# A cross-attention lookup and a two-pass soft mixture of experts on one Trainium2 core: clamped indices, a three-bank routing loop and a bias carried by a weight row

## What is computed

```python
x = x + jnp.tanh(g_xattn[0]) * _L0_xattn_ref(_layernorm(x), itok_S_0_31, ctx_1024)
x = x + jnp.tanh(g_ffn[0]) * _L0_ffn_ref(_layernorm(x), phi_w, phi_b, expert_w, expert_b)

def _L0_xattn_ref(x, layer_idx, weight):
    w = weight[layer_idx]                       # one 128x128 matrix per position
    return jnp.einsum('bsd,sod->bso', x, w)

def _L0_ffn_ref(x, phi_w, phi_b, expert_w, expert_b):
    logits = (jnp.einsum('tzd,ed->tze', x, phi_w) + phi_b).reshape(t, z, n, p)  # n=64, p=32
    D = jax.nn.softmax(logits, axis=3)
    C = jax.nn.softmax(logits, axis=2)
    X_tilde = jnp.einsum('tznp,tzd->npd', D, x)
    X_tilde = jnp.tanh(normalised(jnp.clip(X_tilde, -33000.0, 65000.0)))
    Y_tilde = jnp.einsum('npd,ndH->npH', X_tilde, expert_w) + expert_b[:, None, :]
    return jnp.einsum('tznp,npH->tzH', C, Y_tilde)
```

## Time and profile before

| | |
|---|---|
| median of three runs | 2147.64 us |
| the three runs | 2143.88, 2147.64, 2164.28 us |
| the profiled execution, its own time | 2142.48 us |
| its span in the trace | 2140.7 us |
| mean granted TensorE clock | 0.894 |
| busy: PE / DVE / ACT / POOL | 1713.7 / 1334.7 / 1188.4 / 683.0 us |
| stages A, B1, M, B2 (about) | 0 to 128, 129 to 384, 384 to 425, 425 to 745 us |

### The profile page before, as it was taken

The page is one execution under the profiler, slowest core; times in us unless marked ns, Lnnn a source line. Parts: engine busy times, 40 slices in busy tenths (PEclk is TensorE's granted clock), DMA queues, the critical chain, the costliest instruction groups (busy, mean ns, idle before and its releaser), DMA issues. The chain is left out here.

```text
span 2140.7 us, 40008 instructions
## 1 busy us (share of the span) xinstructions
PE 1713.7 (80%) x12924; PEld 1252.7 (59%) x12924; DVE 1334.7 (62%) x3429; ACT 1188.4 (56%) x4072; POOL 683.0 (32%) x636
## 2 busy tenths in 40 slices
PE   3549999699999839999688865799649998649994
PEld 2425555377877616666487754545526676528883
DVE  4189999377777646667567757312446676674444
ACT  2149999178888618778544432334238888423333
POOL 3035555134444431212034421001300110156774
PEclk9879999599999969999899977799769999659997
DMA  3320000010000024333000022000033432301113
GB/s 109 71 99 1 1 0 1 17 35 1 1 0 1 17 63 109 77 90 100 25 1 0 0 79 83 3 0 0 6 93 95 99 88 68 125 12 46 50 52 138
DMA packets 49332, 99.25 MB, mean 46 GB/s; under 512 B 8842, under 2 KB 16332, under 8 KB 47556
## 3 DMA queue, kind: packets, MB, share of 16 engines
q1 hardware_dynamic: 44548, 87.68, 14.7%
q0 software_dynamic: 4608, 9.32, 1.4%
HBM read 68.14 MB, written 28.77 MB: 45 GB/s over the span
## 5 line engine op out<-in xcount | busy, mean ns | idle before, releaser
L585 ACT ACTIVATE B_E<-B_logits,B_m 128x32 f32<-128x32 f32 (+1 forms) x1792 | 360.2, 362 | 24.1 <-DVE B_m L554 22.6
L592 POOL TENSOR_TENSOR B_E<-B_E,B_r 128x512 f32<-128x512 f32 x256 | 267.7, 1046 | 316.8 <-DVE B_r L573 316.8
L1235 ACT ACTIVATE L_E<-L_sc,L_negm 128x128 f32<-128x128 f32 x1024 | 299.7, 405 | 122.2 <-DVE L_negm L1150 121.7
L1150 DVE TENSOR_REDUCE L_negm<-L_sc 128x4 f32<-128x512 f32 x256 | 174.2, 683 | 127.9 <-PE L_sc L1303 120.2
L554 DVE TENSOR_REDUCE B_m<-B_logits 128x16 f32<-128x512 f32 (+1 forms) x256 | 171.2, 669 | 56.5 <-PE B_logits L548 53.8
L1301 PE MATMUL L_sc<-KS,L_QS 128*128 128x512 f32 x256 | 142.0, 555 | 65.6 <-DMA L_QS<-L_qsplit 53.9
L568 DVE TENSOR_REDUCE B_r<-B_E 128x16 f32<-128x512 f32 (+1 forms) x256 | 172.8, 675 | 11.9 <-ACT B_E L585 10.1
L545 PE MATMUL B_logits<-B_phihi,B_xhi 128*128 128x512 f32 x256 | 156.2, 610 | 22.5 <-ACT B_E L585 10.6
L1243 ACT ACTIVATE L_PT<-L_pt 128x512 f32<-128x512 f32 x256 | 166.9, 654 | 0.6 <-PE L_pt L1311 0.6
L1311 PE MATMUL L_pt<-ident,L_E 128*128 128x128 f32 x1024 | 157.1, 276 | 1.6 <-ACT L_PT L1243 1.6
L1311 PEld LDWEIGHTS L_pt<-ident,L_E 128*128 128x128 f32 x1024 | 123.4, 142 | 24.1 <-ACT L_E L1235 2.0
(11 more groups left out here) (344 smaller groups left out, 3819.3 us busy)
## 6 DMA issues: line engine op xcount, KB each, us to landing
KS<-L_ksplit SPq DMA_DIRECT2D x192, 64.0 KB
L_QS<-L_qsplit SPq DMA_DIRECT2D x48, 256.0 KB, 3.9
F_w<-in_F_w SPq DMA_DIRECT2D x4, 2048.0 KB, 8.5
ew<-in_expert_w SPq DMA_DIRECT2D x1, 4096.0 KB, 14.6
L_cT<-in_ctxT SPq DMA_DIRECT2D x16, 256.0 KB, 4.7
L_ksplit<-L_khi SPq DMA_DIRECT2D x16, 256.0 KB, 2.0
L_ksplit<-L_klo SPq DMA_DIRECT2D x16, 256.0 KB, 2.4
L_qsplit<-L_qhi SPq DMA_DIRECT2D x16, 256.0 KB, 2.7
```

The lines of the kernel that those rows point to most:

```text
L585: ins = nc.scalar.activation(e[:, cols], self.bank(w)[:, cols], ACT.Exp, bias=self.m[:, w % 4, g:g + 1])
L592: self.st.nc.gpsimd.tensor_tensor(e, e, self.r[:, w % 2, :].unsqueeze(2) .to_broadcast([128, self.ng, self.size]), ALU.mult).then_inc(self ...
L1150: nc.vector.tensor_reduce(negm[:, k % 4, :], sc[k % 2][:].rearrange("p (h k) -> p h k", h=NHG), AX.X, ALU.max, negate=True).then_inc(s["ma ...
L1235: ins = nc.scalar.activation(e[:, h * 128:(h + 1) * 128], sc[k % 2][:, h * 128:(h + 1) * 128], ACT.Exp, bias=negm[:, k % 4, h:h + 1])
```

## The change

- Stage A: DVE clamps the indices to 0..31 and multiplies them by 128 once (`itoc`). PE loads 16 values at a time, with no check and no multiplication.
- Both routing passes: units carry one number k = 0..127, everything is written out with no hardware loop, and three logits banks are used as k modulo 3. DVE normalises the next group one sequence per unit (after units 5 to 8 in B1, 3 to 6 in B2). PE transposes after unit 11, ACT splits after unit 12, DVE makes the low half after unit 14.
- B2 gets a ring of eight, `delay` 2 and `LAG` 4, and DVE's finish is spread over units 8 to 11.
- B2's bias matmul is gone. A normalised row sums to zero, so feature 0 may be replaced by 1 when its weight row is subtracted from all rows and the bias put in its place. SP loads the weight row broadcast (`bc`) and the bias at the start of stage M; POOL clears one row of `bc` and subtracts it in four pieces, ahead of the power. The bias parts for B2 in stage A are gone.

```diff
--- before.py
+++ after.py
...
+            v.wait_ge(s["tok_in"], 16)
+            steps.link(nc.vector.tensor_scalar(itoc[:], itok[:], 0, B - 1, ALU.max, ALU.min))
+            nc.vector.tensor_scalar(itoc[:], itoc[:], D, None, ALU.mult).then_inc(s["tok_ready"], 1)
...
-            for h in range(S // 8):
-                _, toks = nc.values_load_multi_w_load_instructions(itok[0:1, 8 * h:8 * h + 8], engines=[mybir.EngineType.PE],
-                                                                   min_val=0, max_val=B - 1)
+            for h in range(S // 16):
+                _, rows = nc.values_load_multi_w_load_instructions(
+                    itoc[0:1, 16 * h:16 * h + 16], engines=[mybir.EngineType.PE], min_val=0, max_val=(B - 1) * D,
+                    skip_runtime_bounds_check_because="VectorE has clamped them")
...
-                                               ctxT[:, bass.ds(toks[4 * (k % 2) + i], 1), :].rearrange("p a o -> p (a o)"),
+                                               table[:, bass.ds(rows[4 * (k % 4) + i], D)],
...
+    def vector_ones(self):
+        for x in self.xn:
+            self.st.nc.vector.memset(x[:, :, 0:1], 1.0)
...
+        q, bank, last = k % NQ, self.bank(k)[:], k - len(self.banks)
+        nc, cols = self.st.nc, slice(q * 512, (q + 1) * 512)
+        if last >= 0 and self.shifted(last):
+            eng.wait_ge(self.diff_done, self.shifts(last))
+        elif last >= 0:
+            eng.wait_ge(self.exp_done, last + 1)
...
-        nc.tensor.matmul(bank, xhi, self.lo[:, cols], start=False, stop=False)
-        nc.tensor.matmul(bank, p.ones16[:], self.bias3[:, cols], start=False, stop=True).then_inc(self.logits_ready, 1)
+        ins = nc.tensor.matmul(bank, xhi, self.lo[:, cols], start=False, stop=self.bias3 is None)
+        if self.bias3 is not None:
+            ins = nc.tensor.matmul(bank, p.ones16[:], self.bias3[:, cols], start=False, stop=True)
+        ins.then_inc(self.logits_ready, 1)
...
-                    if w == LAG and more:
+                if n + 1 < NG:
+                    if w == LAG:
                         v.wait_ge(probs_used, n * UG + soft.RING)
-                        front.vector(v, n + 1, 1 - u)
-                    if w == UG - 4 and more:
-                        front.vector_low(v, n + 1, 1 - u)
+                    if LAG <= w < LAG + GB:
+                        front.vector(v, n + 1, (n + 1) % 2, [w - LAG])
+                    if w == UG - 2:
+                        front.vector_low(v, n + 1, (n + 1) % 2)
...
+            sp.dma_start(bc[:], d["phiT_slots"][0:1, :].to_broadcast([128, NE_L0])).then_inc(bc_in, 16)
+            sp.dma_start(p.phiT[1][0:1, :], d["phi_b_slots"]).then_inc(bias_row_in, 16)
...
+            g.wait_ge(bc_in, 16)
+            nc.gpsimd.memset(bc[0:1, :], 0.0).then_inc(row_set, 1)
+            g.wait_ge(row_set, 1)
+            g.wait_ge(bias_row_in, 16)
+            for q in range(4):
+                cols = slice(q * 512, (q + 1) * 512)
+                nc.gpsimd.tensor_tensor(p.phiT[1][:, cols], p.phiT[1][:, cols], bc[:, cols], ALU.subtract)
             g.wait_ge(var_ready, 1)
...
-    LAG = 3
+    LAG, DELAY = 4, 2
...
-        soft = SoftUnit(st, NL, ct_ready, p.phiT[1], p.bias3[1], 4)
+        soft = SoftUnit(st, NL, ct_ready, p.phiT[1], None, 4, 8, DELAY, 3)
...
+                    if 3 <= w < 3 + GB:
+                        front.vector(v, n + 1, (n + 1) % 2, [w - 3])
+                    if w == UG - 2:
+                        front.vector_low(v, n + 1, (n + 1) % 2)
+                if n:
+                    if w == 8:
+                        mark = add(n - 1)
+                    if w == 9:
+                        steps.need(mark)
+                        mark = tail.row_stats(v, n - 1, (n - 1) % 2, steps)
...
```

More of the change, by code:

```diff
@@ L602, in stage_b1 @@
     LAG, DELAY = 5, 2
+    NU = NG * UG
     with Stage(nc, "B1") as st:
@@ L622, in _ @@
             credit(g, (soft.probs_ready, 2))
-            over_groups_skewed(g, lambda n, u, first, more: [soft.gpsimd(g, n * UG + w, w) for w in range(UG)])
+            for k in range(NU):
+                soft.gpsimd(g, k)
         @block.vector
@@ L654, in _ @@
                     front.scalar(a, 0, 0)
-            def group(n, u, first, more):
-                for w in range(UG):
-                    soft.scalar_exp(a, n, w)
-                    if w == UG - 6 and more:
-                        if not first:
-                            a.wait_ge(soft.logits_ready, n * UG)
-                        front.scalar(a, n + 1, 1 - u)
-            over_groups_skewed(a, group)
+            for k in range(NU):
+                n, w = k // UG, k % UG
+                soft.scalar_exp(a, k)
+                if w == UG - 4 and n + 1 < NG:
+                    if n:
+                        a.wait_ge(soft.logits_ready, n * UG)
+                    front.scalar(a, n + 1, (n + 1) % 2)
         @block.tensor
@@ L814, in _ @@
             credit(g, (soft.probs_ready, 2))
-            def group(n, u, first, more):
-                for w in range(UG):
-                    soft.gpsimd(g, n * UG + w, w)
-                    if w == 10 and not first:
-                        tail.gpsimd(g, n - 1, 1 - u)
-            over_groups_skewed(g, group)
+            for k in range(NU):
+                soft.gpsimd(g, k)
+                if k % UG == 13 and k > UG:
+                    tail.gpsimd(g, k // UG - 1, (k // UG - 1) % 2)
             tail.gpsimd(g, NG - 1, 1)
@@ L839, in finish @@
                     ALU.mult, ALU.add))
-            def group(n, u, first, more):
-                for w in range(UG):
-                    soft.vector(v, n, w, not (first and w == 0))
-                    if w == 4 and more:
-                        v.wait_ge(ct_ready, n * UG + soft.RING)
-                        front.vector(v, n + 1, 1 - u)
-                    if w == UG - 4 and more:
-                        front.vector_low(v, n + 1, 1 - u)
-                    if w == 8 and not first:
-                        finish(n - 1, 1 - u)
@@ L857, in _ @@
+            for k in range(NU - DELAY, NU):
+                soft.vector_sum(v, k)
+                soft.vector_inverse(v, k)
+            steps.need(add(NG - 1))
+            tail.vector(v, NG - 1, 1, steps, None)
         @block.scalar
@@ L924, in _ @@
-            over_groups_skewed(t, group)
-            for w in range(UG, UG + LAG + 1):
-                if w < UG + LAG:
-                    turn((NG - 1) * UG + w - LAG, w - LAG)
-                combine((NG - 1) * UG + w - LAG - 1, w - LAG - 1, 1)
+            for k in range(NU):
+                n, w = k // UG, k % UG
+                if w == 0:
+                    t.wait_ge(front.halves, n + 1)
+                cols = slice(w // NQ * 128, (w // NQ + 1) * 128)
+                soft.tensor_logits(t, k, (front.hi[n % 2][:, cols], front.lo[n % 2][:, cols]), p)
+                if k >= LAG:
+                    turn(k - LAG)
+                if k == LAG + 1:
+                    t.wait_ge(Yt_in, 16)
+                if k > LAG:
+                    combine(k - LAG - 1)
+                if w == UG - 5 and n + 1 < NG:
+                    front.tensor(t, n + 1, (n + 1) % 2, False)
@@ L932 @@
+            for k in range(NU, NU + LAG + 1):
+                if k < NU + LAG:
+                    turn(k - LAG)
+                combine(k - LAG - 1)
 NHG = 4
```

261 lines of the change are left out of this document (122 added, 139 removed).

## The result

The changed kernel took 2069.99 us, the median of four runs (2057.71 to 2083.59), beside 2150.22 us for the kernel before (four runs, 2143.88 to 2164.28). The ratio is 0.9609, with a 95% interval of 0.9567 to 0.9652: faster by 80.2 us. The profiled execution took 2057.71 us, its span is 2055.6 us and the mean granted clock 0.895.

What follows compares the result with a forecast made beforehand. PE was taken to bound A (its sequencer), B1 narrowly and B2, with M waiting for POOL's power. -34.8 - 8.0 + 4.9 - 40.6 + 0.2 = -78.3 us gave 2064.2, raised to 2066; range 2054 to 2088.

Steps and rivals of the forecast that it cites:

- Stage A, -34.8: Stage A's lookup, without checks and multiplications on PE's sequencer, has ACT's last emptying near 66 us, 34.8 us earlier.
- 12 slow positions: Stage A's slow beginning: 12 positions at 0.43 us each, 5.2 us, before the steady 0.22 us a position.
- The seven further loads I cost at nothing: Stage A: PE's loads after the first hide because the sequencer runs ahead; otherwise 8 us come back.
- The lock in each unit: Rival, chance 0.10: in B1 POOL's product holds up each normalisation, making B1 16 us slower and the total 2090 us.
- Stage B1, -8.0: Single normalisations slip in ahead of POOL and PE's 1.10 us hole goes in seven groups: B1 8 us shorter.
- the banks go round by three: B1's logits banks used in turns of three, stated with the spread normalisations and given no time of its own.
- ACT with its 218.6 us holds the banks: The low end for B1: ACT's work, or a late low half, leaves a gain of nothing.
- Stage M, +4.9: POOL's new work ahead of the power makes it start at 398.2 instead of 393.35, 4.9 us more.
- I take 392: Stage M: the time the broadcast lands, chosen between 390.1 at the earliest and 394.5.
- Four subtractions go by POOL's product, 1.05 us each: Stage M: POOL's four subtractions of 512 ahead of the power take 4.2 us.
- Stage B2, -40.4 with the +0.2: B2 without the bias matmul loses 29.2 us, and 11.4 us of waits go; memsets and drain add 0.2.
- The rival that ACT sets the unit: Rival, chance 0.18: in B2 ACT's 2.10 us exceeds PE's 2.04 in unshifted units, making the total 2076 us.

Runs made afterwards that it cites:

- b1_one_piece: The changed kernel with B1's four normalisations of the next group again in one piece after unit 5; stage B1 took 257.70 us against 249.34.
- after_again: The changed kernel measured once more, nothing edited: 2089.2 us, ratio 0.9671 to the kernel before; stage M took 47.49 us.
- m_power_first: The changed kernel with POOL taking stage M's power first, clearing and subtracting after it; stage M took 36.68 us against 39.33.
- b1_old_banks: The changed kernel with B1's low half two units earlier and its banks in the old order 0, 1, 0, 2; stage B1 took 247.06 us.

## Why the prediction was right, and where it wasn't

The forecast of 2066 us lies 4.0 under the median of 2070; the range held it; no rival came true. What it named as the cause was borne out in each stage, but it put no price on the new order of the banks and didn't see the clock in M. How near the total came is partly luck, since the stages behind B2 alone took between 1387 and 1439 us in the profiles. Step by step:

- **Stage A, -34.8: right, -34.5.** PE's first matmul was put at 35.0 and came at 34.96, ACT's last emptying at 65.7 and came at 66.07. Two terms of it missed in opposite ways: 12 slow positions were to cost 2.5 us over the steady pace, and the first 32 took 1.3 us over it; a position takes 0.233 us and not 0.22, 1.6 us over all 128. "The seven further loads I cost at nothing" held nearly: a load of 16 values is 1.7 us long, more than twice that of eight, but 16 positions of PE's work are 3.7. The halved loads, which stand there beside the checks, were no help: with eight values a load stage A is 1.2 to 3.0 us shorter.
- **The lock in each unit: did not happen.** All 28 normalisations took 0.25 us. The row of group 6 with DVE 0.16 us ahead of POOL told this rightly (the kernel after has 169.71 against 169.87 us at such a place), and b1_one_piece shows the price where they aren't spread, 8.4 us. The rival's price was too high all the same: it gave a held normalisation 0.26 + 1.05 = 1.31 us, and the longest took 1.12 to 1.14, so "one product longer" is not what the earlier trace rows say.
- **Stage B1, -8.0: right mechanism, too large; -5.8.** The hole of 1.10 us went. The step that failed is "the banks go round by three", which I had put beside the pieces without a price. It stood among the ends only ("ACT with its 218.6 us holds the banks"). It costs 2.3 us against the old order with the low half early. With both of these B1 is 247.06 us, 8.0 less than before, which is the forecast; so the miss of 2.2 us lies in this step.
- **Stage M, +4.9: mis-sized, +6.5 at the same level over the expert matmuls.** "I take 392" for the broadcast was too early: POOL's clearing starts 8.2 us after the issue, and I had given it 6.6 (other profiles: 7.3 to 7.9). "Four subtractions go by POOL's product, 1.05 us each" was too cheap: they start 1.22 us apart, 0.7 us in all. The stage's own ends, 2.9 and 7.4, held it. The levels are not wholly equal, though: in before PE's first transposes of the stage ran at the lower one too, 3.64 us against 1.94 in after_again. m_power_first, where they took 1.94 us too, has its power 0.9 us sooner after the stage's start than before; with that the cost is nearer 7.4.
- **What stage M then gave back was in no step.** The prediction read the granted clock of the routing passes and called the level safe there, rightly; it never asked at which level M's expert matmuls ran. They ran at the lower one, and 8.2 us hung on that level. Where an execution got the upper level, M came out 1.6 us shorter instead of 6.5 longer.
- **The price of the clock rival was read from a wrong row.** "3.62 us at the low speed" is the first batch of the earlier trace rows, and the granted clock over it was 1.00; why the first positions are slow is not known. The price of 0.88 us per us is near all the same: a later batch that did run at the lower level took 3.61 us (64.93 in the kernel before), and the expert matmuls took 21.0 us against 12.4, 0.69 more per us.
- **Stage B2, -40.4 with the +0.2: -42.8.** Bias: 29.2 expected, 29.8 measured by putting it back. Waits: 11.4 expected, 11.6 for banks, ring, delay and `LAG`, and 1.4 that no run tells apart. The rival that ACT sets the unit was wrong: the unit is 2.03 us, and ACT is busy for 239.4 of 258.6 us.
- **The sum** was right within 7 us for the first profile (-84.6) and within 4.1 for the second (-74.2). The misses of B1 and M (both too optimistic, by 2.2 and 1.6) were made up by B2's 2.4 for the most part, which is luck.

Two things stay open: why the stages behind B2 vary by up to 52 us from one execution to another, and what decides the level of the clock over M's expert matmuls. No run settles either.

## What to carry to other kernels

Before a step of an order of buffers is made uniform, ask for each buffer which engine frees it, and how late: 0, 1, 0, 2 looked odd and was worth 2.3 us over 0, 1, 2 once the low half came early. When work is put ahead of the instruction that a whole stage waits for, first try it behind that instruction, and then look whom it holds up there: here it had to wait for DVE's normalisations as well. And a term that is read from a stretch with pauses needs the granted clock of that stretch, before it is compared with anything.

## What the runs showed of the hardware

- A load of 16 register values took 1.12 to 2.12 us (median 1.69), one of eight 0.59 to 0.60 in the median: more than twice the time for twice the values.
- With one matmul address operation of 37 ns and no check, PE's sequencer keeps up with 128x32 matmuls at 0.23 us a position.
- After a pause of some 18 us in stage M, the same code was granted TensorE's upper level (2.4 GHz) about 4 us after the matmuls began again in two of the three profiles of after, and in the third stayed at the lower (1.2 GHz) for 51 us (351.2 to 402.4).
- In stage B1's group 0, behind a pause of PE of 2.4 us, the granted clock was at the lower level for some 3 us (106.2 to 109.5 in after); with pauses of at most 1.05 us there (b1_old_banks) it stayed at 1.00.
- POOL's subtractions of two full 128x512 operands start 1.22 us apart, its products with a broadcast operand take 1.05 us.
- A broadcast of one row to 128 partitions, 1 MB behind `sel` on one queue, let POOL go on 8.2 us after its issue (7.3 to 8.2 over the profiles in which POOL waits for nothing else), where the plain load of 1 MB landed in 4.7.
